# Vision tower on one core: the second level's patches by gathers instead of picks, all 42 gathers in one piece, another order of the opening

## What is computed

```python
def _level(x, idx, W, b, p, gp):                 # p = 1, 2, 4
    h = H // p
    t = x.reshape(Bsz, C, h, p, h, p).transpose(0, 2, 4, 3, 5, 1).reshape(Bsz, h * h, p * p * C)
    t = t[:, idx]                                # patches along a Hilbert curve
    t = t.reshape(Bsz, h * h // gp, gp * p * p * C)   # 16 patches a group
    return t @ W.T + b

outs = [_level(x, idx, W, b, p, GP) for idx, W, b, p in Ws]       # 256, 64, 16 groups
outs = [outs[0]] + [_interp_linear(o, 256) for o in outs[1:]]
h = concatenate(outs, axis=-1) @ Wf.T + bf
h = h + attention(layernorm(h)); h = h + tree(layernorm(h))
```

## Time and profile before

| | |
|---|---|
| median of 3 runs | 348.1 us (346.37, 348.26, 348.1) |
| profiled execution | 345.99 us, span 344.2 us |
| TensorE (PE) busy | 302.0 us, 88% |
| VectorE (DVE) busy | 229.7 us, 67% |
| ScalarE (ACT) busy | 190.1 us, 55% |
| GpSimd (POOL) busy | 189.7 us, 55% |
| granted TensorE clock, mean | 0.959 |

### The profile page before, as it was taken

How to read it: one execution, slowest core, us unless ns; L and a number is a source line. 1 busy time by engine, 2 the same in 40 slices (tenths; PEclk the granted TensorE clock), 3 DMA queues, 4 the chain that set the end, 5 groups by cost and what they waited for, 6 DMA issues and landing times.

```text
span 344.2 us, 8354 instructions
## 1 busy us (share of the span) xinstructions
PE 302.0 (88%) x2766; PEld 229.3 (67%) x2766; DVE 229.7 (67%) x1136; ACT 190.1 (55%) x395; POOL 189.7 (55%) x411
## 2 busy tenths in 40 slices
PE   0968977488789889999999999999999999999873
PEld 0954974257677756766776776776776677886652
DVE  3101420047549687888889888888898897966882
ACT  1421332034634586586586577577577467758771
POOL 4771047500020386686686686686686686556652
PEclk9995999659999999999999999999999999999997
DMA  7720013100345164165255256254244223000028
GB/s 193 216 37 10 8 32 77 18 0 3 78 114 87 55 88 137 56 91 128 70 85 134 75 84 125 77 85 125 82 83 116 91 82 111 3 4 2 1 80 287
DMA packets 27634, 27.82 MB, mean 81 GB/s; under 512 B 6850, under 2 KB 27328, under 8 KB 27592
## 3 DMA queue, kind: packets, MB, share of 16 engines
q1 hardware_dynamic: 24472, 25.00, 30.7%
q0 software_dynamic: 1184, 1.58, 2.1%
q10 hardware_dynamic: 1936, 0.72, 0.9%
HBM read 4.86 MB, written 3.15 MB: 23 GB/s over the span
## 4 chain that ended last, share of the span: by engine, by line
PE 75%; DVE 6%; another core or an unknown queue 4%; issue 4%; DMA 3%; ACT 3%; SPq 3%; POOL 0%; DVEq 0%; ACTq 0%; POOLq 0%
PE bank L1179 7%; PE bank L1363 7%; PE bank L1397 7%; PE bank L1419 7%; PE bank L1301 4%; PE bank L1320 4%; PE bank L1359 4%; PE bank L1401 4%; PE bank L1337 3%; PE bank L1339 3%; PE bank L1309 3%; PE bank L1422 3%; PE bank L1292 2%; PE bank L1280 2%
## 5 line engine op out<-in xcount | busy, mean ns | idle before, releaser
L877 DVE CUSTOM_DVE_ANT_0 C<-bank,MASKV 128x256 bf16<-128x256 f32 (+1 forms) x384 | 112.4, 351 | 19.1 <-PE bank L1363 14.4
L587 ACT ACTIVATE PT<-bank 128x512 f32<-128x512 f32 x144 | 80.0, 606 | 45.5 <-PE bank L1397 44.0
L382 POOL TENSOR_SCALAR_AFFINE_SELECT PT<-PT 128x256 f32<-128x256 f32 x144 | 66.3, 473 | 0.0
L355 POOL DMA_INDIRECT G<-x,I x32 | 31.2, 974 | 28.8 <-PE bank L1179 19.4
L360 POOL TENSOR_TENSOR PART<-RES,PART 128x256 bf16<-128x256 f32 (+1 forms) x31 | 28.0, 902 | 31.9 <-ACT PART L581 31.9
L378 POOL TENSOR_TENSOR CARRY<-CARRY 1x1 f32<-1x1 f32 x96 | 17.6, 183 | 46.9 <-ACT PT L587 46.9
L1179 PE MATMUL bank<-X,OH 128*128 128x192 f32 x128 | 25.9, 364 | 11.6 <-DMA X<-x 8.0
L1179 PEld LDWEIGHTS bank<-X,OH 128*128 128x128 f32 x128 | 24.2, 215 | 13.1 <-DMA X<-x 8.0
L877 DVE DVE_READ_ACCUMULATOR2_ANT MX<- 128x1 f32 x384 | 31.8, 83 | 0.0
L1419 PE MATMUL bank<-PT,VA 128*32 128x256 f32 x384 | 30.7, 389 | 0.1
L1363 PE MATMUL bank<-KS,QS 96*128 96x256 bf16 x144 | 27.9, 275 | 1.0 <-DVE MX L877 0.8
(11 more groups left out here) (171 smaller groups left out, 680.9 us busy)
## 6 DMA issues: line engine op xcount, KB each, us to landing
QS<-PART SPq DMA_DIRECT2D x72, 96.0 KB, 3.8
KS<-PART SPq DMA_DIRECT2D x72, 96.0 KB, 3.5
out<-HT SPq DMA_DIRECT2D x7, 384.0 KB, 3.6
KSL<-PART SPq DMA_DIRECT2D x24, 96.0 KB, 3.0
QSL<-PART SPq DMA_DIRECT2D x24, 96.0 KB, 3.4
X<-x SPq DMA_DIRECT2D x8, 96.0 KB
G<-x,I POOLq DMA_INDIRECT x34
IR<-ix1r SPq DMA_DIRECT2D x1, 512.0 KB
```

The source lines that it names most:

```text
L355: pool.indirect_dma_start(G0[:, t, F0 * g:F0 * (g + 1), :].rearrange("p f b -> p (f b)"), None, x0, bass.IndirectOffsetOnAxis(ap=I0[:, j:j ...
L382: pool.affine_select(out=e, in_=e, compare_op=ALU.is_ge, fill=0.0, base=0, pattern=[[0, n], [1, P]], channel_multiplier=-1).then_inc(cut_o ...
L587: nc.scalar.activation(PT[:, v, :], BANK[T_BANK[(SU * par + v) % 2]][:, :], ACT.Exp, scale=SCALE).then_inc(exp_ok, 1)
L877: ins = nc.vector.tensor_tensor_reduce(JUNK[:, n:n + keys], bank[:, j * keys:(j + 1) * keys], MASKV[:, S - keys:S], 1.0, LOWEST, ALU.add, ...
```

## The change

- x1's rows come by eight gathers into G1, ahead of G0's 32, with their own index tile I1. SyncE loads I1 between I2 and I0. X1, IR, IOTA, OH, the compares, the picks, and the copies from banks 4 to 7 to G1 are gone.
- GpSimd's wait between the two halves of G0 is gone: 2 + 8 + 32 gathers run in one piece.
- `first_t` waits for the eight gathers and writes banks 4 to 7. TensorE's order is then: E1, all eight sums, patches (0, 0) and (0, 1), tokens (0, 0) and (0, 1), patches (0, 2) and (0, 3), and on as before. ScalarE's and VectorE's queues follow.
- SyncE's last row of ones (KSL) waits for the second E1 product instead of the picks.
- C6 and QSL/KSL change places in SBUF.

```diff
@@ sync
-            for t, src in ((I2, ix2), (I0, ix0)):
+            for t, src in ((I2, ix2), (I1, ix1), (I0, ix0)):
                 sp.dma_start(t[:, :], src).then_inc(ld_idx, 16)
-            sp.dma_start(IR[:, :], ix1r.rearrange("(a n) -> a n", a=1).broadcast_to([P, GP * T1])).then_inc(ld_row, 16)
-            sp.dma_start(IOTA[:, :], iota).then_inc(ld_row, 16)
-            for s in range(CHUNKS):
-                sp.dma_start(X1[:, s, :], x1[s * P:(s + 1) * P, :]).then_inc(x1_in[s], 16)
...
                 if i == RING - 1:
-                    sp.wait_ge(oh_ps, CHUNKS)
+                    sp.wait_ge(pe_a, 10)
@@ gpsimd
-            pool.wait_ge(ld_idx, 32)
+            pool.wait_ge(ld_idx, 48)
             for j in range(2):
                 pool.indirect_dma_start(G2[:, F2 * j:F2 * (j + 1), :].rearrange("p f b -> p (f b)"), None, x2, bass.IndirectOffsetOnAxis(ap=I2[:, j:j + 1], axis=0)).then_inc(g2_in, 16)
+            for j in range(GP // 2):
+                pool.indirect_dma_start(G1[:, F1 * j:F1 * (j + 1), :].rearrange("p f b -> p (f b)"), None, x1, bass.IndirectOffsetOnAxis(ap=I1[:, j:j + 1], axis=0)).then_inc(g1_in, 16)
             for t in range(TT):
-                if t == 1:
-                    pool.wait_ge(oh_ps, CHUNKS)
                 for g in range(GP):
@@ scalar
-            patches_t(0, 0)
-            patches_t(0, 1)
-            for j in (1, 3):
-                act.wait_ge(oh_ps, CHUNKS)
-                nc.scalar.copy(G1[:, 2 * F1 * j:2 * F1 * (j + 1), :].rearrange("p f b -> p (f b)"), BANK[4 + j][:, 0:2 * F1 * B]).then_inc(g1a_ok, 1)
...
+            patches_t(0, 0)
+            patches_t(0, 1)
             tokens(0, 0)
+            tokens(0, 1)
             patches_t(0, 2)
-            tokens(0, 1)
             patches_t(0, 3)
@@ vector
-            dve.wait_ge(ld_row, 32)
-            for s in range(CHUNKS):
-                after(dve, oh_ps, s - OHRING + 1)
-                nc.vector.tensor_scalar(OH[s % OHRING][:, :], IR[:, :], IOTA[:, s:s + 1], None, ALU.is_equal).then_inc(oh_ok, 1)
...
-            dve.wait_ge(oh_ps, CHUNKS)
-            for j in (0, 2):
-                nc.vector.tensor_copy(G1[:, 2 * F1 * j:2 * F1 * (j + 1), :].rearrange("p f b -> p (f b)"), BANK[4 + j][:, 0:2 * F1 * B]).then_inc(g1d_ok, 1)
...
-            sums(0)
-            sums(1)
-            sums(2)
-            sums(3)
+            for q in range(PAIRS):
+                sums(q)
             statistics(0, 0)
-            sums(4)
-            sums(5)
             statistics(0, 1)
-            sums(6)
-            sums(7)
@@ tensor
-            pick(0)
-            pick(1)
             pe.wait_ge(ld_first, 16 * N_FIRST)
...
-            pick(5)
-            pick(6)
-            pick(7)
-            patches_t(0, 0)
-            patches_t(0, 1)
-            pe.wait_ge(g1a_ok, 2)
-            pe.wait_ge(g1d_ok, 2)
-            pe.wait_ge(dve_d, 2)
-            first_t(0)
-            first_t(1)
-            for q in (2, 3):
-                pe.wait_ge(lh_ok, q - 1)
+            pe.wait_ge(g1_in, 16 * GP // 2)
+            for q in range(4):
                 first_t(q)
```

More of the change, by code:

```diff
@@ L20 @@
 BLOCKS = 2 * D // P
-CHUNKS = (IMG // 2) ** 2 // P
-OHRING = 3
 NQ = NT // QD
@@ L107, in vit_tower_kernel @@
         I0 = sb("I0", [P, TT * GP], i32)
+        I1 = sb("I1", [P, GP // 2], i32)
         I2 = sb("I2", [P, 2], i32)
@@ L143, in vit_tower_kernel @@
             G2T = tok("G2T", [2 * F2, GP // 2, B, T2])
-            X1 = tok("X1", [P, CHUNKS, F1 * B])
-            IR = tok("IR", [P, GP * T1], i32)
-            IOTA = tok("IOTA", [P, CHUNKS])
-            OH = [tok(f"OH{i}", [P, GP * T1]) for i in range(OHRING)]
             E1 = tok("E1", [P, B * T1])
@@ L189, in vit_tower_kernel @@
         ld_w6, ld_late, carry_init = sem("ld_w6"), sem("ld_late"), sem("carry_init")
-        ld_row, oh_ok, oh_ps = sem("ld_row"), sem("oh_ok"), sem("oh_ps")
-        x1_in = [sem(f"x1_in{i}") for i in range(CHUNKS)]
-        g1a_ok, g1d_ok = sem("g1a_ok"), sem("g1d_ok")
+        g1_in = sem("g1_in")
         g0_in = [sem(f"g0_in{t}") for t in range(TT)]
@@ L1173, in _ @@
         def _(pe):
-            def pick(s):
-                pe.wait_ge(x1_in[s], 16)
-                pe.wait_ge(oh_ok, s + 1)
-                for j in range(GP // 2):
-                    ins = nc.tensor.matmul(BANK[4 + j // 2][:, (j % 2) * F1 * B:(j % 2 + 1) * F1 * B], OH[s % OHRING][:, j * P:(j + 1) * P], X1[:, s, :],
-                                           start=s == 0 and j % 2 == 0, stop=s == CHUNKS - 1, skip_group_check=True)
-                ins.then_inc(oh_ps, 1)
             def second_t(q):
@@ L1191, in first_t @@
                 for j in range(4):
-                    ins = nc.tensor.transpose(BANK[(2, 3, 0, 1)[q]][0:HALF, j * P:(j + 1) * P], G1[:, :, 4 * q + j], ID[:, :])
+                    ins = nc.tensor.transpose(BANK[4 + q][0:HALF, j * P:(j + 1) * P], G1[:, :, 4 * q + j], ID[:, :])
                 ins.then_inc((pe_d, pe_a)[q % 2], 1)
@@ L1588, in _ @@
             first, second = Image(0, 0), Image(0, 1)
-            sums(0)
+            for q in range(PAIRS):
+                sums(q)
+            patches_t(0, 0)
+            patches_t(0, 1)
+            tokens(0, 0)
+            tokens(0, 1)
             patches_t(0, 2)
-            sums(1)
-            tokens(0, 0)
-            sums(2)
             patches_t(0, 3)
-            sums(3)
-            tokens(0, 1)
-            sums(4)
             tokens(0, 2)
-            sums(5)
             tokens(0, 3)
             patches_t(1, 0)
-            sums(6)
             tokens(1, 0)
-            sums(7)
             tokens(0, 4)
@@ L1771 @@
         "ix0": i0.reshape(TT, P, GP).transpose(1, 0, 2).reshape(P, TT * GP),
+        "ix1": i1.reshape(T1, 2, GP // 2).transpose(1, 0, 2).reshape(P, GP // 2),
         "ix2": i2.reshape(T2, 2, GP // 2).transpose(2, 0, 1).reshape(P, 2),
@@ L1786 @@
         "onesk": np.ones((2, H * S), np.float32).astype(bf16),
-        "ix1r": i1.reshape(T1, 2, GP // 2).transpose(2, 1, 0).reshape(GP * T1),
-        "iota": np.arange(CHUNKS * P, dtype=np.float32).reshape(CHUNKS, P).T,
     }
```

17 lines of the change are left out of this document (6 added, 11 removed).

## The result

| | before | changed |
|---|---|---|
| median, runs of both on the same chip | 347.57 us (20 runs, 343.82 to 350.86) | 349.87 us (20 runs, 347.59 to 351.5) |
| ratio, 95% interval | | 1.0069 [1.0051, 1.0088] |
| profiled execution, span | 345.99, 344.2 | 350.44, 348.7 |
| GpSimd's gathers, start of the first and the last | 4.42, 65.90 | 4.92, 56.34 |
| TensorE's signals free again | 69.80 | 65.17 |

The changed kernel is **slower by 0.7%**; the forecast was 341.5 us, faster. The last gather went out 9.6 us earlier and TensorE's signals came free 4.6 us earlier. But the heads started 5.0 us later, because 24.0 us of work stood behind the release, where 14.4 us had stood before: -4.6 + 9.6 = +5.0. Of this, 4.5 us is left in the span of the profiled executions, and 2.3 us in the medians.

The account below looks back on a forecast made before the run. The opening was taken as bounded by gather trains holding TensorE's signals. Heads 7.9 us earlier less 2.5 charged gave 5.4 us: 345.99 to 340.6, named 341.5 us to allow for repeats; range 334 to 354 for 8 in 10.

Parts of the forecast that it names:

- What bounds the kernel: Opening: a train of gathers holds TensorE's signals back; gain or loss at the first heads passes to the end one for one.
- Gathers and picks: GpSimd and TensorE: 42 gathers in one piece, last issued at 57.3, 8.6 us earlier; dropping 25.9 us of picks worth nothing.
- rival 4: GpSimd: gathers into 128 rows of 768 bytes cost more each, at most 1.8 us; chance 0.12 shared with another rival.
- Release: TensorE's signals all free 3.9 us after the last gather's issue, at 61.2 against 69.80.
- Whether they are through: Opening: whether sums and two patches finish before signals come free; 2.5 us charged against the 7.9 us gain.
- harmless stretch: The first 6 us of a gather train, in which TensorE's signals were taken to be prompt.
- p: Pace per TensorE signal under the train, taken at 2.7 to 3 us.
- rival 2: Opening: slower signal pace leaves the work unfinished when signals come free, about 355 us; chance 0.26 with all that is slower.
- Work behind the release: TensorE, signals free to heads: 14.4 us as before plus 0.7 at half-clock prices, heads at 76.3, gain 7.9 us.
- Clock: TensorE enters the moment of freed signals at 0.50 in both kernels, with the same work behind it; nothing charged.
- Rival 1: Opening: no signals held under the new train, heads at 70.6, gain 13.6 us, about 332 us; chance 0.12.

Follow-up runs that it names:

- e2: The kernel before without GpSimd's wait between its two rows of 16 gathers, 34 gathers in one piece: 353.94 us, ratio 1.0246.
- e4: The kernel before without its wait for the picks, its 32 first-level gathers spaced to 1.55 us by small memsets: 332.19 us, ratio 0.9587.
- e14: The changed kernel with plain DMAs of the same size and queue in place of the 32 first-level gathers, on chip D: 309.75 us, one run.
- e9: The changed kernel as it is, run again on chip C: 349.05 us, ratio 1.01 to the kernel before.
- e7: The changed kernel with its 32 first-level gathers fetching 64 rows instead of 128, on chip B: 328.69 us, one run.
- e17: The kernel before without its wait for the picks, gathers spaced to 1.55 us, run again on chip E: 331.85 us, ratio 1.0032.
- e12: The kernel before without the wait for the picks, 32 columns of zeros behind each first-level gather (step 1.36 us), on chip C: 343.15 us, ratio 0.9934.
- e11: The kernel before without GpSimd's wait for the picks, 34 gathers in one piece, repeated on chip C: 354.35 us, ratio 1.0241.

## Why the prediction was wrong

- *What bounds the kernel: right on the chips that hold signals.* A train of gathers does hold TensorE's signals, and not those of ScalarE and VectorE. e2, e4 and e14 show it by taking away only the pause, adding only the spacing, and removing only the indirection, of 32 of the 42. The opening's loss went through to the end as said: 5.0 us at the heads, 4.5 in the span.
- *Gathers and picks: right.* The last gather was issued at 56.34, against 57.3, and the 128x192 ones cost nothing extra (rival 4 is out). The 25 us of picks were charged at nothing. That holds against the kernel before, where they run while GpSimd pauses or issues; in one piece without a pause they would have stood behind the release (e2).
- ***Release* failed: "All signals are free at 57.3 + 3.9 = 61.2."** I took the delay behind the last issue as a constant because both batches showed about the same, 3.5 and 3.9 us. It grows with the length of the train, as a backlog would: 8.8 us behind the last issue for 42 gathers. The two batches had 18 and 16 gathers, so they could not show the difference between a constant and 0.17 us times the number. Worked per gather, gave 1.41 and 1.44, and 4.9 + 42 x 1.42 = 64.5 for the new train, within 0.7 us of what came. (1.42 lies between them.)
- ***Whether they are through* failed, and it decided: "I take p at 2.7 to 3".** The first signal past the harmless stretch was 16 us late, the next came 11.2 us on, then 6.6, 5.8 and 4.4. By my own bound (p about 4) this is rival 2. At the release 8 of the 24 signals that I had listed were out, where I had all but a few. The pace was read from trains of 16 and 18 gathers, whose end freed everything after 22 to 26 us; nothing there showed what one signal can cost in a longer train, and e2, the same steps as before in a train of 34, has a wait of 31.6 us. "Against it: batch one held about 2 for 13 us" was weighed too high. What sets the single step no run settled.
- *Work behind the release, a size.* Rival 2 had 15.1 + 17.0 = 32.1 us from release to heads, and it was 24.0. I priced the sums and patches that the change adds there at the half clock of the earlier trace rows. The paragraph *Clock* was right that TensorE enters the release at 0.50: e9 shows it, and the 1.00 of the first profile doesn't agree with its own durations. But only the start of the work runs there. In e9 the clock is 1.00 at 73 to 74, in the kernel before it is 0.50 at 75 to 76 and 1.00 at 77 to 78, and what the change adds behind the release runs mostly at the upper level: the sums cost 0.87 us each in the mean instead of 1.54 (6.97 for eight), and tokens 0.77 for four records instead of 1.62. Only E1 went the other way, 3.68 us against the 1.94 of the earlier trace rows, which was a time at the upper level. The two sizes lie on opposite sides, +4.0 for the release and -8.1 for the work, which is why rival 2's 355 was only 5 us above what came. That it came so near is in part luck.

- *Rival 1 (no signals held):* wrong on the chips that hold them. On chip B e7 shows its picture, every signal prompt under 42 dense gathers (32 of them of 64 rows). The Trainium skill, SBUF — State Buffer, section "Who interferes with whom", says DMA never contends with a compute engine. The section speaks of the memory's ports. Read as covering signals too, its rule would have left the train free, and the traces here don't agree: 42 gathers kept one result of TensorE unused for 16 us. Whether it holds for the ports no run here shows.

The version to prefer where signals are held is e4, the kernel before in one piece with a step of 1.55: 332.19 us on chip A where the kernel before takes 346.38. On chip E, which doesn't hold them, the same version (e17) takes 331.85 against 330.71, 0.3% more.

**Open.** The changed kernel itself was not timed on a chip that doesn't hold signals. What the shared path is, why some chips show nothing of it, and why SyncE's issue is slow in some trains were not settled. It is not tied to the late signals: it has its quiet 10.1 us in every run with prompt signals, but in e12 too, where part of the issue fell into the time of held signals. TensorE itself is caught as well: in e2 and e11 its records start 0.70, 1.40, 2.10 or 2.80 us apart while the train holds it, where no wait stands in the program.

## What to carry to other kernels

When an engine idles on a signal whose sender finished long ago, look at what else issues work at that time, and divide the time from its first item to the release by the number of items before you call the delay a constant: two samples of one size can't tell a constant from a rate. A long dense train of indirect DMAs is a resource of its own with a rate (about 1.4 us each here, on three of five chips); issue it clearly slower than that rate (1.55 us was enough in these runs, 1.44 was not), or break it where serial work must pass, and don't add gathers to it to spare an engine that is waiting anyway. Compare kernels within one chip, and repeat what looks settled on a second.

## What the hardware showed that was not expected

- Indirect DMAs from GpSimd at 1.25 us each kept VectorE waiting up to 32.3 us (e11) for a signal of TensorE, and in the changed kernel SyncE's issue of 16 loads took 16.8 us instead of 10.1, while the signals of ScalarE and VectorE there took 0.02 to 0.06 us.
- 64-row gathers did the same as 128-row ones (1.42 and 1.43 us a gather), and plain DMAs at 0.53 us, with the same packets in the same queue, did nothing.
- The rows themselves landed on time all the while: the last packet ended about 2 us behind the start of the last issue whether signals were held or not.
- Five chips fell into two kinds: 330.4 and 330.7 us for the kernel before, or 345.4 to 347.7. With plain DMAs in place of 32 gathers two of them were 4 us apart, instead of 17.
- Spacing of 0.3 us a gather in place of the pause, which ends the train 10.5 us later than without either (e2 to e4), made the kernel 4.1% faster on one kind and 0.3% slower on the other.
